# A second layer whose tokens follow the steps of a scan, with its transposes inside the scan and its scaling on GpSimd

## The reference, cut to what matters

```python
x = x + L0_conv(ln_c(x))      # gated triangular products over k, masked
t = tokens(x)                 # 16384 tokens in order
t = t + L0_ffn(ln_t(t))       # a scan over the tokens, batch 1
x = x + L1_conv(ln_c(x))      # the layer that the change touches
x = tokens(x); x = x + L1_ffn(ln_t(x))   # router, best 2 of 8 experts

# L0_ffn: y = sigmoid(batch_norm(W x_t) + y V^T), step by step
# L1_conv:
zn = layer_norm(z)
a = mask * sigmoid(zn @ w_ag + b_ag) * (zn @ w_ap + b_ap)
b = mask * sigmoid(zn @ w_bg + b_bg) * (zn @ w_bp + b_bp)
p = einsum('bikc,bjkc->bijc', a, b)
out = (layer_norm(p) @ w_z + b_z) * sigmoid(zn @ w_g + b_g)
```

## Time and profile before

| | us |
|---|---|
| median of 3 runs | 323.75 |
| lowest, highest | 322.93, 324.14 |
| profiled execution | 322.78 |
| its span | 321.0 |
| busy in the span: PE | 240.5 |
| DVE | 238.3 |
| POOL | 144.9 |
| ACT | 118.8 |

### The profile page before, as it was taken

One profiled execution on the slowest core, in us unless ns is written; L12 is line 12 of the kernel. 1 busy time (PEld: TensorE's weight loads), 2 busy tenths in 40 slices (PEclk: granted clock), 3 DMA queues, 4 the chain that ended last, 5 costly groups with the idle time before them and its releaser, 6 DMA issues.

```text
span 321.0 us, 4567 instructions
## 1 busy us (share of the span) xinstructions
PE 240.5 (75%) x1504; PEld 170.9 (53%) x1504; DVE 238.3 (74%) x407; ACT 118.8 (37%) x228; POOL 144.9 (45%) x193
## 2 busy tenths in 40 slices
PE   0298986848199799980987995979218799898894
PEld 0176875425044499970566774968218693333331
DVE  4998646978777501029999974789899999798893
ACT  4244334324423166625153652874213241222210
POOL 4405572168600187000034668991963426976200
PEclk9999989887669999997699999999855555999999
DMA  7100000000000000000000000000003881779401
GB/s 227 49 14 1 2 1 0 2 1 0 0 0 0 3 0 0 2 3 0 2 0 0 2 0 0 3 2 0 0 0 84 204 199 40 173 183 205 129 35 65
DMA packets 6636, 13.09 MB, mean 41 GB/s; under 512 B 2774, under 2 KB 3030, under 8 KB 6614
## 3 DMA queue, kind: packets, MB, share of 16 engines
q1 hardware_dynamic: 6470, 12.81, 15.8%
q10 hardware_dynamic: 144, 0.01, 0.0%
HBM read 2.32 MB, written 2.10 MB: 14 GB/s over the span
## 4 chain that ended last, share of the span: by engine, by line
PE 42%; DVE 38%; issue 6%; ACT 6%; POOL 5%; DMA 1%; SPq 0%; DVEq 0%; POOLq 0%; ACTq 0%
PE ps L1315 4%; PE ps L925 4%; DVE sums L324 4%; DVE var L334 4%; PE ps L921 4%; PE ps L985 3%; PE ps L1294 3%; PE ps L1030 3%; POOL x L749 3%; PE ps L549 3%; DVE xn L1781 2%; PE ps L1200 2%; PE ps L1184 2%; DVE gated L1769 2%; PE ps L1307 2%
## 5 line engine op out<-in xcount | busy, mean ns | idle before, releaser
L732 POOL TENSOR_TENSOR gated<-gated,mask_c x16 | 21.0, 1337 | 49.1 <-DVE gated L1769 49.1
L549 PE MATMUL ps<-ident,xn 128*128 128x128 f32 x144 | 28.4, 335 | 16.6 <-DVE xn L538 7.7
L549 PEld LDWEIGHTS ps<-ident,xn 128*128 128x128 f32 x144 | 20.5, 175 | 29.1 <-issue 8.1
L985 PE MATMUL ps<-ones_b,ones_h 128*128 128x512 bf16 x45 | 17.0, 546 | 19.2 <-DVE sums L324 11.6
L749 POOL TENSOR_TENSOR x<-x,sg 128x512 f32 x16 | 22.0, 1388 | 9.1 <-DVE sg L1822 7.6
L330 ACT ACTIVATE squares<-x 128x1024 f32<-128x1024 f32 x16 | 16.9, 1056 | 21.2 <-POOL x L749 11.2
L324 DVE TENSOR_REDUCE sums<-x 128x32 f32<-128x1024 f32 x16 | 19.4, 1212 | 4.1 <-DMA x<-in_x_dram 2.7
L334 DVE TENSOR_REDUCE var<-squares 128x32 f32<-128x1024 f32 (+1 forms) x20 | 22.0, 1102 | 0.0
L956 ACT ACTIVATE gated_t<-ps,bn 128x128 f32<-128x128 f32 x54 | 16.9, 363 | 11.3 <-PE ps L925 10.4
L1294 PE MATMUL ps<-gated,pick 96*128 96x512 bf16 x64 | 20.3, 427 | 0.1
L985 PEld LDWEIGHTS ps<-ones_b,ones_h 128*128 128x128 bf16 x45 | 5.5, 131 | 27.5 <-issue 18.5
(11 more groups left out here) (273 smaller groups left out, 624.9 us busy)
## 6 DMA issues: line engine op xcount, KB each, us to landing
out_gate<-gated SPq DMA_DIRECT2D x32, 128.0 KB, 2.4
x_copies<-gated SPq DMA_DIRECT2D x32, 128.0 KB, 2.4
x<-in_x_dram SPq DMA_DIRECT2D x4, 512.0 KB, 5.9
out_dram<-x SPq DMA_DIRECT2D x8, 256.0 KB, 2.3
e_full<-in_L_ffn_expert_b_dram SPq DMA_DIRECT2D x12, 1.0 KB
mask_a<-in_L_conv_mask_dram SPq DMA_DIRECT2D x1, 64.0 KB, 6.8
mask_c<-in_L_conv_mask_dram SPq DMA_DIRECT2D x1, 64.0 KB, 1.8
w_x<-in_L_ffn_expert_w_dram SPq DMA_DIRECT2D x1, 32.0 KB
```

Source lines behind the costliest of these rows:

```text
L549: ins = pe.transpose(bank(s)[:, t * P:(t + 1) * P], xn[:, s, t, :], ident[:, :])
L732: pool.tensor_tensor(v, v, m.to_broadcast([P, chans, n]), ALU.mult).then_inc(pj.masked, 1)
L985: pe.matmul(bank(b).rearrange("p (k o) -> p k o", o=P), ones_h[:, :], ones_b[:, :].unsqueeze(1).to_broadcast([P, GROUP, P]), start=True, s ...
```

## The change

The second layer takes the tokens of a row in another order. Before, group g held the tokens 16g to 16g+15. Now quarter q holds the tokens whose scan step, within the chunk, is 4q to 4q+3, and group 2q+st holds those of half st of it. Since steps 0 to 3 of the last sweep are finished long before step 15, three of the four quarters are transposed by PE between the steps of the second sweep (behind steps 4, 8 and 12), and DVE adds them to x there. The sums go to a new tensor `x2`, which takes the place of x from there on; x itself then serves as the target of copies for the last layer.

DVE takes the sums, squares and `rstd` of quarter 0 during the sweep, and of quarter 1 up to the sums of squares. `rstd` is now found for a quarter at a time, so four times instead of two. The squares of quarters 0 and 1 are taken by POOL, those of 2 and 3 by ACT. DVE scales groups 0 and 1, POOL scales groups 2 to 7, each before the masks of the group two behind. DVE's work on quarters 2 and 3 is written out between the gates of groups 0 to 3. The mask is copied into the new order (`mask_e`). The five and twelve `idle_products` stand elsewhere. The loops of the sweep have bodies of two steps, five rounds in the first sweep; the second sweep has no loop, and the general path is put into loops.

```diff
+        x2 = sb("x2", [P, P, C])
+        mask_e = sb("mask_e", [P, P])
...
+        def square_of(q):
+            v = x2_q(q).rearrange("p s t c -> p s (t c)")
+            o = squares[:, :].rearrange("p (q s n) -> p q s n", q=QUARTERS, s=2 * S)[:, q, :, :]
+            return o, v
+        def square_c(eng, q):
+            o, v = square_of(q)
+            return eng.tensor_tensor(o, v, v, ALU.mult)
+        def sum_c(dve, q):
+            return dve.tensor_reduce(quarter(sums, q).rearrange("p (s t) -> p s t", t=GROUP), x2_q(q), AX.X,
+                                     ALU.add)
+        def scale_c(eng, q, st, signal, early=False):
+            g = 2 * q + st
+            if not early:
+                eng.wait_ge(p_c.turned, g - 1)
+            src = in_parts(x2, st, q)
+            r = in_order(rstd, st, q)
+            for h in range(2):
+                dst = xn[:, st, 2 * h:2 * h + 2, :].rearrange("p t (r s c) -> p r t s c", r=2, c=C)
+                ins = eng.tensor_tensor(dst, src[:, 2 * h:2 * h + 2, :, :]
+                                        .rearrange("p r (t s) c -> p r t s c", t=2),
+                                        r[:, 2 * h:2 * h + 2, :].unsqueeze(3).to_broadcast([P, 2, GROUP, C])
+                                        .rearrange("p r (t s) c -> p r t s c", t=2), ALU.mult)
+            ins.then_inc(signal, 1)
...
+        n_c = Norm("nc", C, pieces=((0, 32), (32, 64), (64, 96), (96, 128)), **both)
...
-            fused_pool(pool, n_c, mask_gated(p_c, mask_c, 2 * C, 2))
+            for st in range(2):
+                pool.tensor_copy(mask_e[:, :].rearrange("p (q h S t) -> p h q S t", h=2, S=S, t=GROUP)[:, st],
+                                 mask_c[:, :].rearrange("p (S h q t) -> p h q S t", h=2, S=S, t=GROUP)[:, st])
+            for q in range(2):
+                pool.wait_ge(y_added, q + 1)
+                square_c(pool, q).then_inc(n_c.squared, 1)
+            mask_half = mask_gated(p_c, mask_e, 2 * C, 2)
+            for g in range(2, GROUPS + 2):
+                if g < GROUPS:
+                    pool.wait_ge(n_c.done, g // 2 + 1)
+                    scale_c(pool, g // 2, g % 2, p_c.scaled)
+                mask_half(g - 2, g % 2, False)
...
+            if after:
+                for k in range(1, CHUNK):
+                    step(k, k % 2)
+                    if k in after:
+                        after[k]()
+                return
+            step(begin, begin % 2)
+            with pe.Fori((begin + 1) // 2, CHUNK // 2) as it:
+                for b in range(2):
+                    step(2 * it + b, b)
...
+            def turn_y(q, st):
+                to = bank(6 * (q % 2) + st).rearrange("p (S t c) -> p t S c", S=S, c=C)
                 for t in range(GROUP):
-                    ins = pe.transpose(bank(g)[:, t * P:(t + 1) * P], y_cm[:, GROUP * g + t, :], ident[:, :])
+                    ins = pe.transpose(to[:, t, :, :], y_cm[:, CHUNK * st + GROUP * q + t, :], ident[:, :])
                 return ins
+            def turn_quarter(q):
+                if q >= 2:
+                    pe.wait_ge(y_added, q - 1)
+                turn_y(q, 0)
+                turn_y(q, 1).then_inc(y_turn, 1)
+            sweep_pe(pe, s_step, s_state, SWEPT, begun=first_swept,
+                     after={GROUP * (q + 1): lambda q=q: turn_quarter(q) for q in range(QUARTERS - 1)})
             for st in range(2):
                 pe.wait_ge(s_state[st], SWEPT + CHUNK)
-            for g in (0, 1, 2):
-                turn_y(g).then_inc(y_turn, 1)
+            pe.wait_ge(y_added, QUARTERS - 2)
+            turn_y(QUARTERS - 1, 0)
             pe.wait_ge(ends_kept, 2)
-            pe.transpose(bank(6)[0:1, 0:P], dmax[:, :], ident[:, :]).then_inc(flag_turned, 1)
-            for g in (3, 4, 5, 7):
-                turn_y(g).then_inc(y_turn, 1)
+            pe.transpose(bank(2)[0:1, 0:P], dmax[:, :], ident[:, :]).then_inc(flag_turned, 1)
+            turn_y(QUARTERS - 1, 1).then_inc(y_turn, 1)
+            idle_products(3, 5)
...
+            pe.wait_ge(y_added, QUARTERS - 1)
...
-            pe.wait_ge(n_c.summing, 1)
-            idle_products(7, 12)
             groups_held(pe, turn_group(pe, p_c), project_c)
+            idle_products(0, 12)
...
+            def square_late(q):
+                act.wait_ge(y_added, q + 1)
+                o, v = square_of(q)
+                act.activation(o, v, ACT.Square).then_inc(c_squared, 1)
+            square_late(2)
...
+            groups_held_copies(act, copy_c, gates_c, begun=lambda: square_late(3))
...
+            def add_y(q, b, turned, added):
+                dve.wait_ge(turned, q + 1)
+                v = bank(b, 2).rearrange("p (h S n) -> p h S n", h=2, S=S)
+                def part(t):
+                    t = t[:, :, :].rearrange("p (S h q t) c -> p q h S (t c)", S=S, h=2, t=GROUP)
+                    return t[:, bass.ds(q, 1), :, :, :].rearrange("p a h S n -> p (a h) S n")
+                return dve.tensor_tensor(part(x2), part(x), v, ALU.add).then_inc(added, 1)
+            def add_quarter(q):
+                add_y(q, 6 * (q % 2), y_turn, y_added)
+                dve.wait_ge(y_added, q + 1)
+            add_quarter(0)
+            sum_c(dve, 0)
+            chain(dve, take_squares(dve, n_c, 0))
+            take_var(dve, n_c, 0)
+            add_quarter(1)
+            sum_c(dve, 1)
+            dve.wait_ge(n_c.done, 1)
+            scale_c(dve, 0, 0, p_c.scaled, True)
+            chain(dve, take_squares(dve, n_c, 1))
...
+            add_quarter(2)
+            scale_c(dve, 0, 1, p_c.scaled, True)
+            add_quarter(3)
+            take_var(dve, n_c, 1)
...
+            def late_squares(q):
+                dve.wait_ge(c_squared, q - 1)
+                return dve.tensor_reduce(quarter(var, q), quarter_of(squares, q, C), AX.X, ALU.add)
+            sum_c(dve, 2)
+            chain(dve, late_squares(2))
+            gate_c(0, 0)
+            take_spread(dve, n_c, 2)
+            gate_c(0, 1)
+            take_rstd(dve, n_c, 2)
+            gate_c(1, 0)
+            sum_c(dve, 3)
+            gate_c(1, 1)
+            chain(dve, late_squares(3))
+            gate_c(2, 0)
+            take_spread(dve, n_c, 3)
+            gate_c(2, 1)
+            take_rstd(dve, n_c, 3)
+            gate_c(3, 0)
+            gate_c(3, 1)
...
-            fused_dve(dve, n_c, x, y_ready, scale_c, gate_c)
```

More of the change, by code:

```diff
@@ L187, in x_block @@
             first = out_gate[:, :, :].rearrange("p (s n) c -> p s (n c)", s=S)
-            return x_copies[:, :, :] if B % 2 else first
+            second = x[:, :, :].rearrange("p (s n) c -> p s (n c)", s=S)
+            return second if B % 2 else first
         def xr(u):
@@ L282, in build, with chain @@
         block = ctx.enter_context(nc.Block())
[L283 to L289, removed]
+        steps = {dve_step: 0, again_step: 0}
+        def chain(eng, ins, step=dve_step):
+            steps[step] += 1
+            ins.then_inc(step, 1)
+            eng.wait_ge(step, steps[step])
         class Norm:
@@ L941, in sweep_pe, with sweep_act, step @@
                           skip_group_check=True).then_inc(stepped[1], 1)
[L942 to L949, removed]
+            if after:
[8 more added lines that the diff above has]
+                    step(2 * it + b, b)
+        def sweep_act(act, stepped, state, base, first=0, kept=None, looped=False):
+            def step(k, b):
+                for st in range(2):
+                    act.wait_ge(stepped[st], base + k + 1)
+                    act.activation(flat(y_cm, k + CHUNK * st), bank(2 + 2 * st + b)[:, 0:P],
+                                   ACT.Sigmoid, bias=bn[:, 9:10]).then_inc(state[st], 1)
+            if looped:
+                with act.Fori(0, CHUNK // 2) as it:
+                    for b in range(2):
+                        step(2 * it + b, b)
+                return
             for k in range(first, CHUNK):
@@ L1788, in _ @@
-            fused_dve(dve, n_c, x, y_ready, scale_c, gate_c)
+                dve.wait_ge(c_squared, 1)
+                for st in range(2):
+                    dve.wait_ge(r_state[st], (NCHUNKS - 1) * CHUNK)
+                with dve.Fori(0, QUARTERS) as q:
+                    v = y_cm.rearrange("p (h q t) i -> p q h (t i)", h=2, t=GROUP)[:, bass.ds(q, 1), :, :]
+                    dve.tensor_copy(xt[:, :, :, :].rearrange("p h t i -> p h (t i)"),
+                                    v.rearrange("p a h n -> p (a h) n")).then_inc(again_staged, 1)
+                    add_y(q, 0, y_again, again_added)
@@ new lines, in _ @@
+                dve.wait_ge(again_added, QUARTERS)
+                for q in range(2):
+                    sum_c(dve, q)
+                    square_c(dve, q)
+                chain(dve, square_c(dve, 2), again_step)
+                for q in range(2):
+                    chain(dve, take_squares(dve, n_c, q), again_step)
+                for p in range(2):
```

(12 more changed lines are left out.)

140 lines of the change are left out of this document (65 added, 75 removed).

## The result

The kernel after takes 314.47 us (median of 4 runs, 313.46 to 315.67), the kernel before 323.34 beside it (4 runs, 322.80 to 324.14): a ratio of 0.9725, 95% interval 0.9680 to 0.9771. That is 8.9 us less where I had forecast 2.4 less, and it lies under the low end of my range, 316.5. The profiled execution after took 315.67 (span 313.9) against 322.78 (span 321.0), so 7.1 us of the gain can be read in the two traces. The other 1.8 is scatter of the runs: the profiled execution of before lay 0.56 under its median, that of after 1.20 over its own.

A forecast was written before the change was run, and what follows sets the result against it. VectorE, partly waiting for POOL, was taken as the bound. The walk ended at 194.6 against 197.50 us (-2.9); 0.5 for the clock made it -2.4, so 321.3 us was forecast, range 316.5 to 325.8.

The forecast's parts named there:

- the sweeps: Scan's two sweeps: jumps back add 0.44 us and three insertions of eight transposes 2.6, ending the scan 3.05 later.
- DVE up to gate (3, 0): From the first gate at 154.0: 14.0 us of DVE's own work plus 8.0 waiting for POOL, ending at 176.0.
- the clock: Behind the scan, a stretch at half granted clock was expected, adding 0.5 us to the sum.
- DVE during the sweep: Early adds, sums, small steps and scaling under the second sweep: 12.7 us, ending at 142.3, just hidden.
- Rival (d): Early sums not hidden, or the sweep upset by more than 2.6 us: +1 to +3 us, chance 0.10.
- Behind the scan: Scan's end to first gate: transposes 2.1 us, DVE work 5.7, flag and branch 1.3, sums 2.3; gate at 154.0.
- rival (a): POOL and DVE meet less: the 8.0 us go, giving -10, half of it about -6.5; chance 0.15.
- From there to the masks' end: After gate (3, 0): POOL 3.8 us, PE's projections and transposes 11.4, last gates and mask 3.4, ending at 194.6.
- keep-busy products: Twelve products moved behind the last projection: 2.6 us inside 3.4 of waiting, so no cost.
- Rival (b): POOL's half scalings at 0.9 us and the branch at 2.0: +0.6 us, 324.4, no change; chance 0.15.
- Rival (c): Granted clock falls in the dense part from 180 us on: slower, 324.9 to 331 us; chance 0.10.

The follow-up runs named there:

- unrolled kernel: The kernel after with the first sweep's ten looped steps written out; 314.23 us, ratio to before 0.9725, and 313.72 us, 0.9685, when repeated.
- few masked: The kernel after with masks of groups 0 to 2 laid on only 4 of 64 channels; 311.31 us, ratio to before 0.9635.
- both edits joined: The kernel after with POOL scaling and masking one group earlier and the first sweep's steps written out; 310.38 us, ratio to before 0.9580.
- Turned late: The kernel after with the three quarters turned, added and normed only behind the second sweep; 324.45 us, ratio to before 1.0036.

## Why the prediction was wrong, step by step

The mechanism and the chain were right. Four terms of the sum were too large: the sweeps (with their start), the way to the first gate, DVE up to gate (3, 0) and the clock. The one that matters is *DVE up to gate (3, 0)*, with 3.0 of the 4.7 us. Forecast 194.6 for the first product transpose and 0.5 for the clock, measured 190.38 and 0: 4.7 us, the whole of 7.1 - 2.4. They lie as follows.

**The sweeps, 3.05 forecast, 2.56 measured.** Three insertions of 0.87 are the 2.6 that I had. The loops cost not +0.44 but nothing: the first sweep, 110.98 to 124.61, is 0.8 longer than before, and the second, now written out, takes 0.9 less without its turns (17.27 - 2.61 against 15.56). The price of a jump was right: a step of the first sweep takes 0.99 to 1.00 in the loop and 1.23 to 1.28 over a jump, so 0.24 to 0.29 against the 0.22 of the earlier trace rows. What I had left out is that a written-out step takes 0.95, so that the second sweep gains on every step. Both together are the 1.52 of the unrolled kernel: about 1.0 for four jumps and 0.5 for the steps. With the sweep's start 0.22 earlier, the sweeps make 0.7 of the error.

**DVE during the sweep** was hidden, as forecast: the last sum of squares ends at 141.09, and `dif` waits for ACT at 142.00. POOL's squares took 1.89 instead of the 2.5 that I took. Rival (d) is out.

**Behind the scan.** The flag came 2.06 us after it (2.1). Adds, scaling and eleven steps took 5.5 (5.7). Reading the flag and branching cost DVE 0.94, in the open, where I had taken 1.3 within 0 to 2.0. The chain of waits tells the load of the flag (L1867) from the branch (L1868), with the sum behind it starting at 150.41:

```profile
149.47 0.37 DVEq L1867
149.87 0.22 DVEq L1867
...
150.20 0.06 DVEq L1868
```

So the load took 0.73 and the branch with what follows it 0.21. The Trainium skill, Advanced Engine Details and Errata, Control Flow Timing, has 0.11 us for a compare-and-branch; the 0.21 holds the start of the next instruction too and doesn't speak against it. Most of what I had to price was the load. From the scan's end to the first gate it was 10.9 and not 11.4, 0.5 of the error, and the first gate came at 152.79, not 154.0.

**DVE up to gate (3, 0): the step that failed.** Forecast 14.0 of own work and 8.0 of waiting, 22.0; measured 171.77 - 152.79 = 18.98. The waits, each small step's time over its 0.19, are 0.97, 1.67, 1.37 and 1.64 for the four runs of steps: 5.65. I had taken 1.3, 2.5, 1.7 and 2.5, the full length of POOL's instructions, and put the small steps' own time on top. But a step that waits out a mask runs inside that mask's time, and one that stands between two scalings runs inside them too: for `rstd` of quarter 2, DVE is held from 156.59 to 158.90, 2.31 us, and three steps of 0.22 are done in it, so that only 1.65 is added. Moreover in three of the four runs the first two steps slip in, since POOL's mask starts some 0.2 us behind the first of them (153.90 against 153.66). This is a part of rival (a), which I had at 0.15: of its 8.0 us 2.35 went, less than a third. That the -7.1 of the traces lies near the -6.5 that I gave for half of it is luck, since the other terms make up the difference. I argued against it that POOL's instructions follow each other without a pause. Where a mask and the scalings meet they do, but a pause isn't needed. The Trainium skill, SBUF — State Buffer, Who interferes with whom, says that a DVE instruction with two SBUF inputs and a GpSimd one that reads SBUF exclude each other for the whole instruction, and that whoever issues first has it; the rows of 150 to 159 agree, and few masked shows that these waits are on the chain (4.3 us). `take_spread`'s L378 waits too, though it reads one tensor only; the same section counts `tensor_scalar` among the operations that can take both ports. So 2.35 of the 3.0 us are the waits, and what remains is DVE's own work, 13.3 instead of 14.0.

**From there to the masks' end.** 171.77 to 175.56 is 3.79 (3.8). PE, from 175.56 to the end of its last projection at 187.02, takes 11.5 (11.4), and from there it is 3.4 to 190.38 (3.4). A half scaling takes 0.60. The keep-busy products cost nothing, as forecast. Rival (b), POOL dearer, is out.

**The clock.** I had added 0.5 for a stretch at the lower level; there was none. Rival (c) did not happen in the kernel after. A fall did come in the unrolled one, at 150 to 162, and cost 0.6 there; so the term was not absurd, but the sparse part of this kernel didn't bring the clock down. Why it fell there and not with both edits joined stays open. In the kernel before, the granted clock was 0.81, 0.50 and 0.83 in the three windows from 144 to 162, where it is 1.00 now. That is no part of the gain: DVE worked there from 143.99 to 163.9 without a gap, so it waited for nothing of PE's.

**What the change is worth, by part.** The stretch is 9.46 shorter and the sweep 2.56 longer, 6.9 net. Turned late, the change is worth nothing at all (+0.4%); the scaling on POOL gives 1.4. I had not written out how much the early start alone would be worth, and so did not see that the gain rests on it.

## What to carry to other kernels

When two engines exclude each other per instruction, add up the time in which either works, not the sum of the waiting engine's own time and the other's: short steps run inside the time they wait. An order in which the engine that feeds the next stage scales one group earlier can be worth more (2.6 us here) than moving the scaling to it at all (1.4). And compare parts of a profile between fixed points, since a start that scatters by 2 us hides gains of 1.

## What the runs showed of the hardware that I had not expected

A square of 1,024 elements on POOL, where both inputs are the same tensor, takes 1.89 us, while a product of 512 elements of two tensors takes 1.28 and one of 256 takes 0.61, so the cost isn't in proportion; whether the size or the shared input makes it is not shown. A run through the flag and past the skipped block costs DVE 0.94 us, in both profiles of the kernel after, 0.73 of it the load. Ten steps of the scan in a loop of two-step bodies cost TensorE 1.52 us more than the same ten written out: some 0.25 for each jump back and 0.05 for each step. And the unrolled kernel had the granted clock fall behind the scan in two profiles of two: if each window mixes 1.00 and 0.50, about 6.8 and 3.4 us were spent at the lower level of 1.2 GHz.
